# Experts in blocks of 256 rows, with the first layer's weights as the stationary operand

## The reference

```python
shared = _gelu(t @ sw1 + sb1) @ sw2 + sb2
probs = jax.nn.softmax(t @ gate_w + gate_b, axis=-1)
topk_p, topk_i = jax.lax.top_k(probs, K)
combine = jnp.zeros((T, E), t.dtype).at[jnp.arange(T)[:, None], topk_i].set(topk_p)
h = _gelu(jnp.einsum('td,edf->etf', t, w1) + b1[:, None, :])
y = jnp.einsum('etf,efd->etd', h, w2) + b2[:, None, :]
routed = jnp.einsum('te,etd->td', combine, y)
return (routed + shared).reshape(Bb, Ss, Dm)
```

## Time and profile before

| what | value |
|---|---|
| median of 3 runs | 2069.25 us (2067.45 to 2070.11) |
| the profiled execution's own time | 2068.23 us |
| its span, first to last instruction | 2066.5 us |
| busy in the span: PE, DVE, ACT, POOL | 93%, 73%, 68%, 50% |
| chain that ended last: PE, ACT, DVE | 83%, 11%, 2% |
| mean granted clock of TensorE | 0.982 |

### The profile page before, as it was taken

One profiled execution on the slowest core, in us unless ns is written; L12 is line 12 of the kernel. 1 busy time (PEld: TensorE's weight loads), 2 busy tenths in 40 slices (PEclk: granted clock), 3 DMA queues, 4 the chain that ended last, 5 costly groups with the idle time before them and its releaser, 6 DMA issues.

```text
span 2066.5 us, 39929 instructions
## 1 busy us (share of the span) xinstructions
PE 1928.5 (93%) x14653; PEld 1519.9 (74%) x14653; DVE 1506.6 (73%) x2786; ACT 1414.9 (68%) x2169; POOL 1029.5 (50%) x1197
## 2 busy tenths in 40 slices
PE   6899999999999999999999999999999974998998
PEld 5676767676767676767676777777777753998998
DVE  5577777777778787878787878787777665665565
ACT  6877777777777777777777777777777742444444
POOL 4444555555555545454545464646464643444444
PEclk9999999999999999999999999999999996999999
DMA  3000000000000000010101010101010125664664
GB/s 134 1 11 11 32 22 32 21 32 21 28 25 26 27 21 32 17 36 15 38 11 42 11 42 11 42 11 42 11 42 1 42 85 167 198 190 133 193 180 140
DMA packets 74653, 112.53 MB, mean 54 GB/s; under 512 B 10713, under 2 KB 53214, under 8 KB 74464
## 3 DMA queue, kind: packets, MB, share of 16 engines
q1 hardware_dynamic: 59456, 67.88, 11.3%
q0 software_dynamic: 15008, 42.10, 5.5%
HBM read 63.09 MB, written 48.65 MB: 54 GB/s over the span
## 4 chain that ended last, share of the span: by engine, by line
PE 83%; ACT 11%; DVE 2%; issue 1%; DMA 1%; POOL 0%; SPq 0%; POOLq 0%; DVEq 0%
PE bank_o L1230 12%; PE ring L1209 7%; PE ring L1136 6%; PE ring L1137 6%; PE ring L1142 6%; PE ring L1214 6%; PE ring L1188 6%; ACT prob L599 3%; PE acc L1253 3%; PE acc L1261 3%; PE acc L1255 3%; PE ring L1195 3%; ACT prob L605 2%; PE bank_d L1244 2%; PE ring L1398 2%; PE ring L1399 2%
## 5 line engine op out<-in xcount | busy, mean ns | idle before, releaser
L515 POOL TENSOR_SCALAR_AFFINE_SELECT prob<-prob 128x256 f32<-128x256 f32 x512 | 229.7, 470 | 544.3 <-ACT prob L605 544.1
L599 ACT ACTIVATE prob<-ring 128x1024 f32<-128x1024 f32 (+1 forms) x384 | 326.4, 875 | 199.9 <-PE ring L1214 196.6
L527 POOL TENSOR_TENSOR key_sum<-prob 128x768 f32<-128x768 f32 x128 | 242.2, 1892 | 212.6 <-PE bank_d L1244 200.2
L605 ACT ACTIVATE prob<-prob 128x1024 f32<-128x1024 f32 (+1 forms) x384 | 342.7, 916 | 5.3
L1230 PE MATMUL bank_o<-prob,v 128*32 128x512 f32 (+3 forms) x4096 | 307.1, 441 | 16.6 <-issue 7.5
L798 DVE TENSOR_TENSOR kT<-ring,kT 64x512 fp32r<-64x512 f32 x256 | 176.2, 688 | 166.9 <-ACT kT L612 164.2
L1209 PE MATMUL ring<-qT,kT 128*128 128x256 f32 (+3 forms) x1024 | 240.0, 336 | 54.4 <-ACT qT L622 19.7
L1209 PEld LDWEIGHTS ring<-qT,kT 128*128 128x128 f32 x1024 | 166.6, 191 | 135.7 <-issue 59.1
L1230 PEld LDWEIGHTS bank_o<-prob,v 128*32 128x32 f32 x4096 | 118.2, 111 | 177.5 <-issue 160.0
L814 DVE RECIPROCAL norm<-bank_d 128x512 f32<-128x512 f32 x64 | 214.9, 3358 | 25.7 <-PE bank_d L1244 24.1
L1214 PE MATMUL ring<-q_lo,kT 128*128 128x256 f32 (+3 forms) x1024 | 229.2, 326 | 1.0 <-DVE q_lo L803 0.9
(11 more groups left out here) (218 smaller groups left out, 4673.5 us busy)
## 6 DMA issues: line engine op xcount, KB each, us to landing
xin<-first SPq DMA_DIRECT2D x71, 257.0 KB, 3.1
xin<-second SPq DMA_DIRECT2D x71, 129.0 KB, 2.5
xin<-base SPq DMA_DIRECT2D x71, 128.0 KB, 2.6
x_next<-in_x SPq DMA_DIRECT2D x16, 512.0 KB, 4.7
x_res<-in_x SPq DMA_DIRECT2D x16, 512.0 KB, 4.0
raw_e<-in_w SPq DMA_DIRECT2D x4, 1024.0 KB, 6.7
first<-pad SPq DMA_DIRECT2D x9, 257.0 KB, 4.4
second<-pad SPq DMA_DIRECT2D x9, 129.0 KB, 6.2
```

What stands on the lines that cost most here:

```text
L515: last = nc.gpsimd.affine_select(out=diag, in_=diag, compare_op=ALU.is_ge, fill=0.0, base=0, pattern=[[0, 2], [1, P]], channel_multiplier=-1)
L527: nc.gpsimd.tensor_tensor(sums[:, :, :], t0[:, :, P:N], t13[:, :, 0:N - P], ALU.add).then_inc(sum_steps, 1)
L599: nc.scalar.activation(probs[p % PROBS][u][:, :, :], slot[:, :, 0:UNIT_COLS[u]], ACT.Tanh, scale=SCALE / SOFTCLAMP).then_inc(act_emptied, 1)
L605: nc.scalar.activation(cols, cols, ACT.Exp, scale=SOFTCLAMP).then_inc(exp_done, 1)
```

## The change

Experts now take blocks of 256 rows, two tiles each. An expert's rows are rounded up to whole blocks, so TILES is 2 x (32 + 7) = 78 for each choice, 156 in all, 78 blocks. The rest follows from that:

- `turn_in(b)` waits for two loads and makes 4 transpositions into one bank.
- In `expert_hidden(b)` the weights are the stationary operand and the 256 tokens stream, so the hidden layer comes out already transposed, and `turn_hidden` is gone. The stationary operand needs a fixed place: VectorE (`fetch_high`) and ScalarE (`fetch_low`) copy the expert's first weights into `w1_of` for each block, in two sets; each of them reads the table for that. 12 products of 256 columns.
- The bias b1 is added in `activate`, as the bias of the activation, in two instructions of 256 columns, one for each half of the hidden layer. Before the stage TensorE spreads the biases to `b1_of` by four small products with `owner`, which says whose tile each one is.
- `act_high` and `act_low` read `act_out` in SBUF; they read PSUM before.
- `expert_out(b)` is as before for each of the two tiles, 14 products; block b's results alternate between `acc` and `ring[1]`.
- The list of VectorE has three more steps for the table, and LAG is 5.

XIN, YOUT, the scatters and the waits of the loads for them stay. In the diff the lines taken out are mostly left out (they are among the functions above):

```diff
-TILES = TOKENS // P + E - 1
+PAIR = 2
+BLOCK = PAIR * P
+TILES = PAIR * (TOKENS // BLOCK + E - 1)
...
+            xinT = [[sb(f"xinT{k}{s}", [P, DC, BLOCK], F32R, arena) for s in ("h", "l")] for k in range(2)]
+            act_out = [sb(f"act_out{k}", [P, FC, BLOCK], F32, arena) for k in range(2)]
+            pad = sb("pad", [P, ROW], F32, arena)
+            actT = [[sb(f"actT{k}{s}", [P, FC, BLOCK], F32R, arena) for s in ("h", "l")] for k in range(2)]
+            w1_of = [[sb(f"w1_of{k}{s}", [P, DC, FF], F32R, arena) for s in ("h", "l")] for k in range(2)]
+            b1_of = sb("b1_of", [P, K, FC, P], F32, arena)
...
+        def y_bank(n):
+            return (acc, ring[1])[n // PAIR % 2][:, n % PAIR, 0:D]
+        def weights_of(engine, b, known):
+            k, j = TILE[PAIR * b]
+            starts_at = nc.values_load_multi_w_load_instructions(
+                table[K + k:K + k + 1, j:j + BATCH], engines=(engine,), min_val=0, max_val=(E - 1) * D,
+                skip_runtime_bounds_check_because="an expert's number below 8 times 256, or zero")[1]
+            known.update({b + m // PAIR: at for m, at in enumerate(starts_at)
+                          if m % PAIR == 0 and j + m < TILES})
...
-            LAG = 2
+            LAG = 3 * PAIR - 1
...
+            def in_high(b):
+                act.wait_ge(turned, b + 1)
+                if b >= 2:
+                    act.wait_ge(h_full, b - 1)
+                bank = (bank_o, bank_d)[b % 2]
+                nc.scalar.copy(xinT[b % 2][0][:, :, :],
+                               bank[:, :].rearrange("p (c t) -> p c t", c=DC)).then_inc(in_hi, 1)
+            def activate(b):
+                k, j = TILE[PAIR * b]
+                act.wait_ge(h_full, b + 1)
+                if b >= 2:
+                    act.wait_ge(act_lo, b - 1)
+                for f in range(FC):
+                    last = nc.scalar.activation(act_out[b % 2][:, f, :], ring[0][:, b % 2, f * BLOCK:(f + 1) * BLOCK],
+                                                ACT.Gelu, bias=b1_of[:, k, f, j:j + 1])
+                last.then_inc(h_done, 1)
+            def act_high(b):
+                act.wait_ge(h_done, b + 1)
+                if b >= 2:
+                    act.wait_ge(y_full, PAIR * (b - 1))
+                nc.scalar.copy(actT[b % 2][0][:, :, :], act_out[b % 2][:, :, :]).then_inc(act_hi, 1)
+            act.wait_ge(b1_spread, 1)
+            nc.scalar.copy(b1_of[:, :, :, :], ring[1][:, 0, :].rearrange("p (k f j) -> p k f j", k=K, f=FC)
+                           ).then_inc(b1_ready, 1)
+            act.wait_ge(b1_ready, 1)
+            weights_at_block = {}
+            def fetch_low(b):
+                if TILE[PAIR * b][1] % BATCH == 0:
+                    weights_of(mybir.EngineType.Activation, b, weights_at_block)
+                if b >= 2:
+                    act.wait_ge(h_full, b - 1)
+                nc.scalar.copy(w1_of[b % 2][1][:, :, :],
+                               w_e1[1][:, :, bass.ds(weights_at_block[b], FF)].bitcast(F32)).then_inc(fetched[1], 1)
+            count = len(TILE) // PAIR
+            act.wait_ge(e_lo, 4)
+            for b in range(2):
+                in_high(b)
+                fetch_low(b)
+            for b in range(count):
+                if b + 2 < count:
+                    in_high(b + 2)
+                if b + 1 < count:
+                    activate(b + 1)
+                act_high(b)
+                if b + 2 < count:
+                    fetch_low(b + 2)
...
+            then(nc.vector.tensor_scalar(blocks_of[:, :, :], tiles_of[:, :, :], 1.0 / PAIR, 0.25, ALU.mult, ALU.add))
+            then(nc.vector.tensor_scalar(blocks_of[:, :, :], blocks_of[:, :, :], 2.0 ** 23, None, ALU.add))
+            then(nc.vector.tensor_scalar(blocks_of[:, :, :], blocks_of[:, :, :], 2.0 ** 23, float(PAIR),
+                                         ALU.subtract, ALU.mult))
-                                         tiles_of[:, :, None, :].to_broadcast(shape), ALU.mult))
+                                         blocks_of[:, :, None, :].to_broadcast(shape), ALU.mult))
+            nc.vector.tensor_copy(owner[:, :, :], bank_o[0:E, P:(K + 1) * P].rearrange("p (k j) -> p k j", k=K)
+                                  ).then_inc(owner_ready, 1)
...
+            def in_low(b):
+                dve.wait_ge(in_hi, b + 1)
+                bank = (bank_o, bank_d)[b % 2]
+                nc.vector.tensor_tensor(xinT[b % 2][1][:, :, :], bank[:, :].rearrange("p (c t) -> p c t", c=DC),
+                                        xinT[b % 2][0][:, :, :].bitcast(F32), ALU.subtract).then_inc(in_lo, 1)
+            def act_low(b):
+                dve.wait_ge(act_hi, b + 1)
+                nc.vector.tensor_tensor(actT[b % 2][1][:, :, :], act_out[b % 2][:, :, :],
+                                        actT[b % 2][0][:, :, :].bitcast(F32), ALU.subtract).then_inc(act_lo, 1)
+                nc.vector.scalar_tensor_tensor(y_out[n % YOUT][:, :], y_bank(n),
+            weights_at_block = {}
+            def fetch_high(b):
+                if TILE[PAIR * b][1] % BATCH == 0:
+                    weights_of(mybir.EngineType.DVE, b, weights_at_block)
+                if b >= 2:
+                    dve.wait_ge(h_full, b - 1)
+                nc.vector.tensor_copy(w1_of[b % 2][0][:, :, :],
+                                      w_e1[0][:, :, bass.ds(weights_at_block[b], FF)].bitcast(F32)
+                                      ).then_inc(fetched[0], 1)
+            count = len(TILE) // PAIR
+            dve.wait_ge(e_hi, 4)
+            dve.wait_ge(table_ready, 1)
+            for b in range(2):
+                fetch_high(b)
+                in_low(b)
+            for b in range(count):
+                if b + 2 < count:
+                    in_low(b + 2)
+                    fetch_high(b + 2)
+                act_low(b)
+                if b >= 1:
+                    for t in range(PAIR):
+                        weigh(PAIR * (b - 1) + t)
+            for t in range(PAIR):
+                weigh(PAIR * (count - 1) + t)
...
+                         ident[:, :])
+            for k in range(K):
+                last = pe.transpose(bank_o[0:E, (k + 1) * P:(k + 2) * P], found[:, 2, k, :], ident[:, :])
+            last.then_inc(table_turned, 1)
+            pe.wait_ge(owner_ready, 1)
+            pe.wait_ge(b1_loaded, 16)
...
+            last.then_inc(b1_spread, 1)
+            def turn_in(b):
+                for n in range(PAIR * b, PAIR * (b + 1)):
+                    pe.wait_ge(xin_loaded[n % XIN], 16 * (n // XIN + 1))
+                if b >= 2:
+                    pe.wait_ge(in_lo, b - 1)
+                bank = (bank_o, bank_d)[b % 2]
+                for t in range(PAIR):
+                    for c in range(DC):
+                        last = pe.transpose(bank[:, c * BLOCK + t * P:c * BLOCK + (t + 1) * P],
+                                            xin[(PAIR * b + t) % XIN][:, TOKEN + c * P:TOKEN + (c + 1) * P],
+                                            ident[:, :])
+            weights_at_block = {}
+            def expert_hidden(b):
+                if TILE[PAIR * b][1] % BATCH == 0:
+                    weights_of(mybir.EngineType.PE, b, weights_at_block)
+                tokens = xinT[b % 2]
+                pe.wait_ge(fetched[0], b + 1)
+                pe.wait_ge(fetched[1], b + 1)
+                pe.wait_ge(in_hi, b + 1)
+                if b >= 2:
+                    pe.wait_ge(h_done, b - 1)
+                dsts = [ring[0][:, b % 2, f * BLOCK:(f + 1) * BLOCK] for f in range(FC)]
+                weights = [[[w[:, c, f * P:(f + 1) * P] for w in w1_of[b % 2]] for c in range(DC)] for f in range(FC)]
+                for f in range(FC):
+                    for c in range(DC):
+                        pe.matmul(dsts[f], weights[f][c][0], tokens[0][:, c, :], start=f == 0 and c == 0, stop=False)
+                        pe.matmul(dsts[f], weights[f][c][1], tokens[0][:, c, :], start=False, stop=False)
+                pe.wait_ge(in_lo, b + 1)
+                for f in range(FC):
+                    for c in range(DC):
+                        last = pe.matmul(dsts[f], weights[f][c][0], tokens[1][:, c, :], start=False,
+                                         stop=f == FC - 1 and c == DC - 1)
+                last.then_inc(h_full, 1)
+            def expert_out(b):
+                at, hidden_hi, hidden_lo = weights_at_block[b], actT[b % 2][0], actT[b % 2][1]
+                pe.wait_ge(act_hi, b + 1)
+                if b >= 2:
+                    pe.wait_ge(y_ready, PAIR * (b - 1))
+                pe.wait_ge(act_lo, b + 1)
+                for t in range(PAIR):
+                    dst, here = y_bank(PAIR * b + t), slice(t * P, (t + 1) * P)
+                    for f in range(FC):
+                        for w in w_e2:
+                            pe.matmul(dst, hidden_hi[:, f, here], w[:, f, bass.ds(at, D)],
```

(14 more changed lines are left out.)

## The result

The changed kernel takes 2111.49 us (median of 4, 2109.30 to 2114.48), the kernel before 2069.68: 1.0201 times as long, 95% interval 1.0185 to 1.0217. That is +41.8 us where +37 was forecast (2106, range 2062 to 2136). The profiled execution took 2109.30 us with a span of 2107.2, 40.7 more than before.

The account below looks back on a forecast made before the run. TensorE bounds the kernel now; after the change the ring of 12 xin tiles, only 6 blocks, would make it wait. Ring and stage +32.0, scatters +7, clock +5, start -6.6: +37, 2106 us, range 2062 to 2136.

Parts of the forecast that it names:

- TensorE's instructions in a round: TensorE, each two-tile block: 4 transpositions, 12 hidden and 14 output products, 3.51 us; 78 blocks make 273.8 against 299.6 before.
- load to turning: Landing of a row load in xin before turn_in: 3.1 us in the first choice, 2.5 in the second.
- three rounds: Loop through the 12 xin tiles: three rounds at least 13.2 or 12.3 us, where TensorE wants 10.5.
- scatters lengthened by VectorE: GpSimd's scatters lose time under act_low or fetch_high, two-input or copy steps in SBUF: 0.3 us a pass, 23 passes, +7.
- clock in the rounds: TensorE's clock halves after idle time in one pass of three rounds in nine: +5 us, bounds 0 and 43.
- start of the stage: Before the experts: the last scatter of first escapes L1093's subtractions, so TensorE starts earlier, -6.6 us; if caught, +1.4.
- The last rival: TensorE's clock falls in most passes and every scatter is caught: 2140 to 2165 us; chance 0.09.
- the rule taken in full: GpSimd contends with every two-SBUF-input VectorE instruction: every pass pays 1.2 us, making the scatter term 28.
- the base of 312.2: Experts stage in the kernel before: both choices and the gap between them, 312.2 us, which the forecast stage time was compared with.
- TensorE alone: Rival in the experts stage: buffers return fast enough, so TensorE still decides; -26, 2043 us; chance 0.04.
- ScalarE's queue: Rival: hidden product waits for fetch_low behind activate and act_high; 3.73 us a round, -9, 2061 us; chance 0.05.
- At nothing: Terms put at no cost: fetch_high, fetch_low, longer copies, table reads, b1 load and products, fewer bias transfers, later base loads.

## Why the prediction was right, step by step

| step | forecast | measured |
|---|---|---|
| TensorE's instructions in a round | 3.51 | 3.50 (with VectorE's copy and 16 buffers) |
| hidden product to the second scatter | 4.60 | 4.75 (median of 64) |
| scatter to the load that waited, first / second choice | 3.6 / 3.3 | 3.0 / 3.2 (mean, second of each pair) |
| load to turning | 3.1 / 2.5 | 3.5 / 3.2 (the same tiles) |
| three rounds | 13.2 / 12.3 | 13.39 / 13.27 (by the stretches of 37 and 35 rounds 13.14 / 13.32) |
| scatters lengthened by VectorE | +7 | 0: median 0.97, mean 0.98 |
| clock in the rounds | +5 | at most +7: four falls of 3.4 us |
| idle at the hand-over | about 8 | 9.05 |
| start of the stage | -6.6 | -6.0 |

**What held.** The buffers decide, and the waits fall where they were expected: at turn_in, behind loads that follow scatters, three rounds to a pass. The rounds with 10 and 12 buffers, and with 6 in the old kernel, follow from one loop of 13 to 14 us (10 for a single tile) shared by two or three rounds; with 14 and 16 its share is under the 3.66 us at which something else decides. The start came out as forecast, on a margin of 0.14 us. The clock was sized about right: it fell four times in the 72 rounds, for 3.4 us each, with TensorE busy all the while, so each fall cost 1.7 us at most; in the kernel before it fell only at the first filling and at the hand-over. The last rival, a fall in most passes, did not come. Two of the four falls, and the kernel before:

```profile
1828.03:1831.45 3.42, 3.42 (x19) 3.42 (x18) 1.45 (x3) 1.90 (x5) 0.71 (x1) 0.50 0.95 277
2022.59:2026.01 3.42, 3.42 (x18) 3.42 (x18) 1.45 (x3) 1.94 (x5) 0.85 (x1) 0.50 0.67 212
...
1755.89:1904.80 148.91, 148.90 (x1274) 148.69 (x1272) 90.42 (x212) 72.03 (x212) 67.85 (x70) 1.00 0.61 179
1916.32:2061.10 144.78, 144.25 (x1234) 144.05 (x1232) 88.07 (x206) 68.97 (x203) 67.06 (x69) 1.00 0.60 176
```

**What failed.** Two terms were mis-sized in opposite directions, and that they nearly cancel is luck. In the second choice the landing was sized at 2.5 us from single loads of before; behind a wait it is 3.2, and with the 0.15 on the second scatter three rounds are 13.27 instead of 12.3, three of the four falls of the clock among them: about 1 us x 35 / 3 = +11. Against that, the scatters lost nothing. The prediction let a scatter lose whatever part of act_low or fetch_high it meets, and took its 0.97 beside one PSUM input from rows in which no scatter starts under a subtraction. It is the start that counts. In 36 blocks of the changed kernel act_low started inside a scatter, which stayed at 0.97, as act_low did at 0.69; the two scatters that started under act_low took 1.24 and 1.05. In GpSimd's and VectorE's timelines, one of either kind:

```profile
1788.58 0.98 POOL L585 DMA_INDIRECT base<-y_out,xin  x1 [0.30 <-issue]
1789.09 0.69 DVE L1152 TENSOR_TENSOR actT1l<-act_out,actT1h 128x512 fp32r<-128x512 f32 x1 [1.18 <-ACT actT1h L739]
...
2015.17 0.69 DVE L1152 TENSOR_TENSOR actT0l<-act_out,actT0h 128x512 fp32r<-128x512 f32 x1 [1.70 <-ACT actT0h L739]
2015.47 1.24 POOL L590 DMA_INDIRECT out_dram<-y_out,xin  x1 [2.25 <-issue]
```

fetch_high held a scatter that started under it too, by less: up to 1.08 in eight cases. The 48 that started under in_low, one input from PSUM, at least 0.15 before its end, took 1.03 at most. In the changed order a first scatter starts 1.2 us after act_low has ended (1851.65 against 1850.46), so scatters seldom start under it; with weigh ahead nearly all first ones do (1.22 on the mean). The Trainium skill (GPSIMD Engine Reference, section 8, Key points) says that GpSimd contends with VectorE's instructions that have two SBUF inputs; that run agrees with it, with 1.46 against 0.97 for the scatter that starts under act_low, and the sum by the rule taken in full, 28 us, does not hold for the changed kernel.

The sum over all: the 78 rounds were put at 336.9 us (28.1 + 296.8 + 7 + 5) and took 338.6 (317.5 for 72, the other six at 3.51). Filling, hand-over and drain, put at 19.3, took the other 25.7 of the 364.3; but the base of 312.2 ends at 2061.10 and leaves out the 5.4 us behind it today, so the two make 1.0 together.

**The rivals.** TensorE alone was put at 2043; with 16 buffers, VectorE's copy and the longer lead between the choices it is 2043.7, though 9 us of that come from the lead, which the figure did not contain. ScalarE's queue was put at 3.73 us a round and 2061, deciding only where the ring is faster; with 16 buffers it was 3.66 and 2060.2. "At nothing" for fetch_low was right at 12 buffers and no longer at 16.

**What stays open.** Why the loads come back later when the scatters move forward, and what holds ScalarE's activation for 1.2 to 3.2 us in the fast rounds.

## What to carry to other kernels

When a change makes a block larger, count the buffers in blocks: the time from a buffer's last use to its next, divided by the rounds between the two, is a bound for the round, and it is read from the waits of today's trace even where they cost nothing. When that bound is lifted, the next loop stands close behind; here it was a 0.6 us copy on another engine, off every critical path as long as the buffers decided. Where a place in an order decides what lies beside what, moving an instruction out of a loop can lengthen its neighbours; look at their durations, and at which of two started first.

## What the runs showed of the hardware

- An indirect scatter of 0.97 us took 9.65 and 10.17 us when it started under the first of eight back-to-back subtractions with two SBUF inputs, and 1.46 when it started 0.07 us into one such subtraction of 0.69. Where the subtraction started inside the scatter, both kept their time (36 cases). Started under a copy of 0.42 from SBUF it took up to 1.19; under a subtraction whose other input is in PSUM, 1.03 at most.
- In all six runs with 14 or 16 buffers an activation of ScalarE, that of block 61, started 1.6 to 3.2 us after everything that it waits for was there; in three of them it was the same at every second block behind it. The profile puts some of these waits down to "remote"; the cause is not known.
- A product behind transpositions can be late by 0.1 us without any idle time in the profile, because the modelled end of the transpositions covers it; the length of the round showed it.
